# TensorE multiplies zeros in 32-row by 64-column tiles while the first rows load

## The chip, the cores and the metric

The kernel runs as one program on one core of a Trainium2 chip. The metric is the device time in microseconds (us) of that core, as the median of several runs. Beside it stands one profiled execution, from which all rows below are taken. TensorE (PE in the rows; its weight loads are PEld), VectorE (DVE), ScalarE (ACT), GpSimd (POOL) and SyncE (SP, which issues the DMAs here) each run their own instruction stream and meet at semaphores.

## The reference, cut to what matters

Two layers, each an attention-like part and a mixture of experts, over x of 4 sequences x 1024 rows x 256 columns:

```python
x = L0_attn_x                                   # (4, 1024, 256), float32
xn = _layernorm(x, axis=-1)
s = _L0_attn_ref(xn, ...)                       # layer norm again, Q, K, V, cumulative sum, gate
g = _silu(_L0_ffn_ref(xn, ...))                 # 16 experts by top-k of softmax(xn @ gate_w.T), and a shared one
x = x + s * g
xn = _layernorm(x, axis=-1)
s = _L1_attn_ref(xn, ...)                       # causal attention, 16 heads of 64, rotary positions
g = _silu(_L1_ffn_ref(xn, ...))                 # 8 experts, top 2
x = x + s * g
```

The change lies ahead of the first `_layernorm`. The zeros that it multiplies are used by nothing.

## The kernel before, in words

`build` runs stages one after the other: `normalize` (both layer norms of layer 0, and the gate's logits), `first_layer`, `experts`, `attention`, `moe`, `attention`. Between stages all engines meet at a barrier. Only `normalize` is changed; it takes the first 52 us.

`normalize` works in four batches b of 8 tiles of 128 rows (batch 0 in two halves), with these streams, each in written order:

- SP issues the loads: two halves of batch 0 of x (L162), four constants (L164), three more batches of x (L166). Later it issues the stores of the normalized rows (L173) and the loads of layer 0's weights (L170).
- VectorE, per batch: `statistics` (L190, L193, L196), then `rescaled` of the batch before (L220), then `staged` of its own (L209). `rescaled(b)` waits for `scaled_ps` 4b (L216), which TensorE raises when it has turned the scaled tiles of batch b-1; `staged` waits for GpSimd's reciprocal roots and, from batch 2 on, for `stage_ps` 4(b-1). In the end it copies the logits (L238).
- GpSimd computes the roots (L253 to L257, L268 to L270).
- TensorE, per batch: `turn_stage` (16 transposes of 128x128 by multiplication with the identity, L290), `logits` (8 x 2 multiplications, L299), `turn_scaled` (16 transposes, L310). Its first instruction waits for the four constants (L273 to L275), then `turn_stage` waits for `stage_made`.
- ScalarE evicts the turned tiles from PSUM (L326, L332).

A float32 multiplication by data appears in the trace as two weight loads and two MATMUL records; a transpose appears as one of each. A multiplication whose operands start at partition 0, 32, 64 or 96 and whose output covers only part of the partitions uses only that part (tile) of the array. `attention` does this for its heads: L1539 uses tiles of 64 rows by 128 columns, L1561 of 128 rows by 64 columns, L1571 of 64 rows by 128 columns; in each two tiles alternate.

`Scope.start` raises every semaphore of a stage by one, shared out over the five engines in turn, and then lets all engines meet. `normalize` has 20 of them before the change, four per engine.

Of the kernel before, what the change touches and what calls it, by code (L numbers as in the profile page):

```python
# [16 lines left out]
P = 128  # L17
# [9 lines left out]
ONE = 1  # L27
# [5 lines left out]
HEADS, DH = 16, 64  # L33
INNER = HEADS * DH
PAIRS = HEADS // 2
TB = T // P
# [82 lines left out]
def tiles(ap, n=TC):  # L119
    return ap.rearrange("p (t c) -> p t c", t=n)  # L120

def normalize(nc, d):
# [3 lines left out]
    with ExitStack() as ctx:  # L127
        s = Scope(nc, "n0", ctx)
# [11 lines left out]
        ps = s.banks()  # L140
# [5 lines left out]
        stage_ps, stage_read, scaled_ps, scaled_read = (s.sem(n) for n in ("stage_ps", "stage_read", "scaled_ps", "scaled_read"))  # L146
        log_ps, xn_out = s.sem("log_ps"), s.sems("xn_out")
        LOG = ps[6:8]

        def rows8(dram, b):  # L150

            return dram[b * T:(b + 1) * T, :].rearrange("(t p) c -> p t c", p=P)
# [5 lines left out]
        with nc.Block() as block:  # L158
            @block.sync
            def _(sp):  # L160
                for half, sem in ((0, x_half), (1, x_in[0])):
                    sp.dma_start(tiles(x[:, half * HT * C:(half + 1) * HT * C], HT), rows_of(d.x, half)).then_inc(sem, 16)  # L162
                for dst, src in ((ident, d.ident), (gate_w, d.gate_w["n0"]), (gain, d.gain["n0"]), (off, d.off["n0"])):
                    sp.dma_start(dst[:, :], src).then_inc(consts, 16)  # L164
                for b in range(1, QT):
                    sp.dma_start(tiles(part(x, b), GT), rows8(d.x, b)).then_inc(x_in[b], 16)  # L166
                for b in range(QT):
                    if b == 2:
                        for dst, src in d.l0_loads:
                            sp.dma_start(dst[:, :], src).then_inc(d.l0_in, 16)  # L170
                    u = b % 2
                    sp.wait_ge(stage_made, b + 2 + ONE)
                    sp.dma_start(rows8(d.xn["n0"], b), tiles(stage[u][:, :], GT)).then_inc(xn_out[u], 16)  # L173
                for u in range(2):
                    sp.wait_ge(xn_out[u], 16 * QT // 2 + ONE)
                sp.wait_ge(d.l0_in, 16 * len(d.l0_loads) + ONE)

            @block.vector
            def _(dve):
                st = Steps(dve, steps)  # L180

                def do(ins):
                    st.done(ins)
                    st.wait()

                def statistics(n):
                    at, wide = PARTS[n]
                    cols = slice(at, at + wide)
                    for i in range(at, at + wide):
                        st.done(dve.bn_stats(stats[:, i * 6:i * 6 + 6], x[:, i * C:(i + 1) * C]))  # L190
                    st.wait()
                    for i in range(at, at + wide):
                        st.done(dve.bn_aggr(mv[:, i * 2:i * 2 + 2], stats[:, i * 6:i * 6 + 6]))  # L193
                    st.wait()
                    var = mv[:, :].rearrange("p (t m) -> p t m", m=2)[:, cols, 1]
                    dve.tensor_scalar(v[:, cols], var, EPS, None, ALU.add).then_inc(var_made, 1)  # L196

                def staged(n):
                    at0, wide = PARTS[n]
                    b = at0 // GT  # L200
                    u = b % 2
                    dve.wait_ge(r_made, n + 1 + ONE)
                    if b >= 2:
                        dve.wait_ge(xn_out[u], 16 * (b // 2) + ONE)
                        dve.wait_ge(stage_ps, 4 * (b - 1) + ONE)
                        dve.wait_ge(scaled_made, b - 1 + ONE)
                    for at in range(at0, at0 + wide):
                        i = at % GT
                        ins = dve.tensor_scalar(stage[u][:, i * C:(i + 1) * C], x[:, at * C:(at + 1) * C],  # L209
                                                mv[:, 2 * at:2 * at + 1], r[:, at:at + 1], ALU.subtract, ALU.mult)  # L210
                    ins.then_inc(stage_made, 1)

                def rescaled(b):
                    u = b % 2
                    dve.wait_ge(r2_made, b + 1 + ONE)
                    dve.wait_ge(stage_made, b + 2 + ONE)  # L216
                    dve.wait_ge(scaled_ps, 4 * b + ONE)
                    for i in range(GT):
                        at = b * GT + i
                        ins = dve.tensor_scalar(scaled[u][:, i * C:(i + 1) * C], stage[u][:, i * C:(i + 1) * C],  # L220
                                                r2[:, at:at + 1], None, ALU.mult)
                    ins.then_inc(scaled_made, 1)

                dve.wait_ge(x_half, 16 + ONE)
                statistics(0)
                dve.wait_ge(x_in[0], 16 + ONE)
                statistics(1)
                staged(0)
                staged(1)
                for b in range(1, QT):  # L230
                    dve.wait_ge(x_in[b], 16 + ONE)
                    statistics(b + 1)
                    rescaled(b - 1)
                    staged(b + 1)
                rescaled(QT - 1)
                dve.wait_ge(log_ps, QT + ONE)
                for b in range(QT):
                    dve.tensor_copy(d.logits[:, :].rearrange("p (i b e) -> p b i e", b=B, e=E0)[:, b],  # L238
                                    LOG[b // 2][:, b % 2 * GT * E0:(b % 2 + 1) * GT * E0].rearrange("p (i e) -> p i e", e=E0))

# [31 lines left out]

            @block.tensor  # L273
            def _(pe):
                pe.wait_ge(consts, 16 * 4 + ONE)  # L275

                def xn_turned(b, i, c):
                    at = c * N + b * T + i * P
                    return xnT[:, at:at + P]

                def turn_stage(b):
                    for j in range(4):
                        half, c = j // 2, j % 2
                        if c == 0:
                            pe.wait_ge(stage_made, (1 + half if b == 0 else b + 2) + ONE)
                        if 4 * b + j >= 3:
                            pe.wait_ge(stage_read, 4 * b + j - 2 + ONE)
                        for i in range(4):
                            at = (half * 4 + i) * C + c * P
                            last = pe.transpose(ps[(4 * b + j) % 3][:, i * P:(i + 1) * P], stage[b % 2][:, at:at + P], ident[:, :])  # L290
                        last.then_inc(stage_ps, 1)

                def logits(b):
                    for i in range(GT):
                        if i % 4 == 0:
                            pe.wait_ge(stage_read, 4 * b + 2 * (i // 4) + 2 + ONE)
                        at = (b % 2 * GT + i) * E0
                        for c in range(KC):
                            last = pe.matmul(LOG[b // 2][:, at:at + P], xn_turned(b, i, c), gate_w[:, c * P:(c + 1) * P], start=c == 0, stop=c == KC - 1)  # L299
                    last.then_inc(log_ps, 1)  # L300

                def turn_scaled(b):
                    pe.wait_ge(scaled_made, b + 1 + ONE)
                    for j in range(4):
                        half, c = j // 2, j % 2
                        if 4 * b + j >= 3:
                            pe.wait_ge(scaled_read, 4 * b + j - 2 + ONE)
                        for i in range(4):
                            at = (half * 4 + i) * C + c * P
                            last = pe.transpose(ps[3 + (4 * b + j) % 3][:, i * P:(i + 1) * P], scaled[b % 2][:, at:at + P], ident[:, :])  # L310
                        last.then_inc(scaled_ps, 1)

                for b in range(QT):
                    turn_stage(b)
                    logits(b)
                    turn_scaled(b)
# [24 lines left out]
def renormalize(d, s, ps, gel, gel_done, stage, scaled, turned):  # L341
# [23 lines left out]
    scaled_late = s.sem("scaled_late")  # L365
    LOG = ps[7]

# [33 lines left out]
    def vector(dve):  # L401
# [56 lines left out]
        dve.wait_ge(log_ps, G + ONE)  # L458
        dve.tensor_tensor(out=te(d.sc), in0=LOG[:, 0:W].rearrange("p (t e) -> p t e", e=E1), in1=over_t(br), op=ALU.add)
        late_evicted(G - 1)  # L460
# [32 lines left out]
    def tensor(pe):  # L493
# [9 lines left out]
        def logits(g):  # L503
            pe.wait_ge(stage_read, 2 * g + 2 + ONE)
            for i in range(GT):
                at = (g * GT + i) * E1
                for c in range(KC):
                    last = pe.matmul(LOG[:, at:at + P], turned[g % 2][c][:, i * P:(i + 1) * P], gate_w[:, c * P:(c + 1) * P],
                                     start=c == 0, stop=c == KC - 1)
# [1685 lines left out]
```

## Time and profile before

| | us |
|---|---|
| three runs | 2538.72, 2538.75, 2542.49 |
| median | 2538.75 |
| span of the profiled execution, from first to last instruction | 2537.7 |
| TensorE busy in it | 2427.7 (96%) |
| VectorE, ScalarE, GpSimd busy | 1315.6, 1106.0, 606.3 |
| first MATMUL starts | 12.32 |
| last MATMUL of `normalize` ends | 50.23 |

The span is 1.05 us short of the median, which is what lies around the program. The mean granted clock of TensorE over the span is 0.982 of full speed. A busy time is the union of its records, so two records that run beside each other count once. The chain of waits of the page covers only 12% of the span and none of `normalize`, so for this stage the order of time and the waits of each engine are read instead.

### The profile page before, as it was taken

Reading aid. Unit: us, or ns where it says so; the run is one execution under the profiler, and the core shown is the slowest. Engines: PE = TensorE matmul, PEld = TensorE weight load, DVE = VectorE, ACT = ScalarE, POOL = GpSimd, SP = SyncE. Lnnn points to the kernel's source line nnn. Section 1 sums busy time; section 2 is a strip of 40 time slices with the busy share of each in tenths; the row PEclk is TensorE's granted clock in tenths of the full one; section 3 lists DMA queues with packets and bytes.
Section 4 is the critical chain, followed back from the end, with each engine's and each line's share of the span. In section 5 each row is a group of like instructions: output and inputs, shape, how many; then the busy total and the mean of one; then the engine's idle time right before and its main releaser. Section 6 shows DMA issues by size and latency. Waiting matters only on the chain. (4 is left out here: it accounts for less than half of the span.)

```text
span 2537.7 us, 45251 instructions
## 1 busy us (share of the span) xinstructions
PE 2427.7 (96%) x14680; PEld 1710.2 (67%) x14681; DVE 1315.6 (52%) x3690; ACT 1106.0 (44%) x2581; POOL 606.3 (24%) x535
## 2 busy tenths in 40 slices
PE   6999998999987899999999999999999999799997
PEld 5555555655566566666666666666899999566665
DVE  6666241222246766666666666655333333366665
ACT  3211111111125566666666666666222222266665
POOL 3002001444445233432111111110111111134341
PEclk9999999999988999999999999999999999899999
DMA  6013103975446232332111222122767666324231
GB/s 213 17 50 116 50 17 108 274 213 161 116 125 218 63 98 81 106 97 73 40 35 42 58 67 56 44 58 78 252 234 244 234 243 234 107 73 128 90 96 59
DMA packets 133965, 296.05 MB, mean 117 GB/s; under 512 B 16864, under 2 KB 87024, under 8 KB 123472
## 3 DMA queue, kind: packets, MB, share of 16 engines
q1 hardware_dynamic: 112896, 251.59, 31.0%
q0 software_dynamic: 20944, 42.94, 6.4%
q8 instruction: 60, 0.98, 0.2%
q14 instruction: 65, 0.53, 0.1%
HBM read 193.80 MB, written 67.12 MB: 103 GB/s over the span
## 5 line engine op out<-in xcount | busy, mean ns | idle before, releaser
L1595 ACT ACTIVATE at_p<-at_p,at_nmax 128x640 f32<-128x640 f32 (+7 forms) x512 | 392.5, 767 | 179.5 <-DVE at_nmax L1804 177.7
L1630 POOL TENSOR_TENSOR kept_big<-kept_xg 128x1024 f32<-128x1024 f32 x64 | 151.0, 2359 | 899.5 <-DVE kept_xg L1824 899.5
L1602 ACT ACTIVATE at_pT<-at_ps 128x512 f32<-128x512 f32 (+1 forms) x640 | 311.3, 573 | 106.2 <-PE at_ps L1547 106.1
L1804 DVE CUSTOM_DVE_ANT_0 at_p<-at_ps,atk_mask 128x512 f32<-128x512 f32 (+3 forms) x512 | 281.8, 585 | 143.7 <-PE at_ps L1539 143.5
L1547 PEld LDWEIGHTS at_ps<-kept_ident,at_p 128*128 128x128 f32 x2304 | 257.7, 142 | 111.5 <-issue 60.2
L1547 PE MATMUL at_ps<-kept_ident,at_p 128*128 128x128 f32 x2304 | 304.4, 278 | 11.4 <-ACT at_p L1595 10.8
L1539 PE MATMUL at_ps<-kept_big 64*128 64x512 f32 (+3 forms) x1536 | 298.7, 507 | 10.2 <-POOL kept_big L1630 6.5
L1561 PE MATMUL at_ps<-at_pT,at_v 128*64 128x256 f32 (+1 forms) x2560 | 270.2, 362 | 2.5 <-issue 2.5
L1839 DVE SCALAR_TENSOR_TENSOR kept_big<-at_ps,at_inv,kept_big 128x256 f32<-128x256 f32 x512 | 214.1, 475 | 89.1 <-issue 67.8
L1524 PE MATMUL at_ps<-atk_h,atk_w 128*128 128x512 f32 x512 | 240.8, 604 | 17.8 <-SPq L1338 17.8
L1561 PEld LDWEIGHTS at_ps<-at_pT,at_v 128*64 128x64 f32 x2560 | 174.0, 137 | 116.1 <-issue 29.3
L1038 PE MATMUL ex_ps<-kept_big 128*128 128x512 f32 x480 | 211.0, 598 | 0.9 <-ACT kept_big L1095 0.9
L1944 PEld LDWEIGHTS moe_ps<-moe_xT,moe_w 128*128 128x128 f32 x1696 | 197.5, 192 | 3.8 <-ACT moe_xT L1977 0.7
L1944 PE MATMUL moe_ps<-moe_xT,moe_w 128*128 128x128 f32 x1696 | 198.1, 275 | 0.5 <-ACT moe_xT L1977 0.5
L1539 PEld LDWEIGHTS at_ps<-kept_big 64*128 64x128 f32 x1536 | 128.3, 188 | 82.8 <-issue 47.6
L1038 PEld LDWEIGHTS ex_ps<-kept_big 128*128 128x128 f32 x480 | 92.1, 192 | 111.1 <-issue 110.4
L1100 ACT ACTIVATE kept_big<-ex_ps 128x512 f32<-128x512 f32 x64 | 38.2, 597 | 291.2 <-PE ex_ps L1038 269.0
L1524 PEld LDWEIGHTS at_ps<-atk_h,atk_w 128*128 128x128 f32 x512 | 92.1, 195 | 99.2 <-issue 80.9
L1922 POOL DMA_INDIRECT z_rows<-late_yo,late_to x71 | 68.8, 969 | 374.4 <-DVE late_yo L2005 374.4
L1804 DVE CUSTOM_DVE_ANT_0 at_p<-at_ps,atk_mask,at_nmax 128x128 f32<-128x128 f32 (+3 forms) x256 | 135.1, 546 | 27.9 <-PE at_ps L1539 27.9
L1824 DVE TENSOR_TENSOR kept_xg<-kept_xg,atk_cos 128x1024 f32<-128x1024 f32 x64 | 78.1, 1220 | 127.3 <-DMA kept_xg<-kept_xg 127.3
L1124 DVE TENSOR_TENSOR kept_big<-kept_big,ex_ps 128x512 f32<-128x512 f32 x64 | 44.0, 687 | 188.0 <-ACT kept_big L1100 188.0
(244 smaller groups left out, 3419.2 us busy)
## 6 DMA issues: line engine op xcount, KB each, us to landing
moe_w<-in_w_w SPq DMA_DIRECT2D x53, 1028.0 KB, 4.8
kept_xg<-kept_xg SPq DMA_DIRECT2D x256, 128.0 KB, 2.3
atk_first_w<-in_w_w SPq DMA_DIRECT2D x18, 1028.0 KB, 4.8
atk_w<-in_w_qkv SPq DMA_DIRECT2D x32, 384.0 KB, 3.1
slot_in<-kept_big SPq DMA_DIRECT2D x9, 1032.0 KB, 9.4
kept_big<-in_w_eg SPq DMA_DIRECT2D x16, 512.0 KB, 3.5
kept_big<-in_w_eu SPq DMA_DIRECT2D x16, 512.0 KB, 5.0
kept_big<-in_w_ed SPq DMA_DIRECT2D x16, 512.0 KB, 6.9
```

The costliest lines, as they stand in the source:

```text
L1038: last = pe.matmul(bank, w[:, k * F0 + f * P:k * F0 + (f + 1) * P], xT[u][k][:, :], start=k == 0, stop=k == KC - 1)
L1524: last = pe.matmul(banks[0], w[x][:, k * QKV + m * P:k * QKV + (m + 1) * P], h[:, k * T + half * CH:k * T + (half + 1) * CH], start=k == 0 ...
L1539: pe.matmul(banks[e][:, 0:to - at], qkT[x][e * DH:(e + 1) * DH, n * P:(n + 1) * P], qkT[x][e * DH:(e + 1) * DH, T + at:T + to], start=True ...
L1547: last = pe.transpose(banks[0][:, (i - 4 * j) * P:(i - 4 * j + 1) * P], p[(2 * t + e) % LAG][:, k * P:(k + 1) * P], ident[:, :])
L1561: last = pe.matmul(banks[0][e * DH:(e + 1) * DH, skip:QW], v[x][:, (k * 2 + e) * DH:(k * 2 + e + 1) * DH], pT[n][:, at + skip:at + QW], st ...
L1595: act.activation(buf, buf, ACT.Exp, bias=nmax[:, unit:unit + 1], scale=-1.0, accum_out=rsum[:, unit:unit + 1]).then_inc(exp_done, 1)
L1602: act.activation(dst, ring[RING_BANK[part][ev]][:, 0:(i1 - i0) * P].rearrange("p (k c) -> p k c", c=P), ACT.Copy).then_inc(t_read, 1)
L1630: pool.tensor_tensor(out=qkT[x][:, :].rearrange("p (m t) -> p m t", m=2)[:, :, half * CH:(half + 1) * CH], in0=raw[half][:, :].rearrange(" ...
L1804: ins = dve.tensor_tensor_reduce(out=p[unit % LAG][:, at:to], in0=ring[RING_BANK[part]["S", ((t, c), e), ahead]][:, 0:to - at], in1=mask[: ...
L1824: dve.tensor_tensor(out=both, in0=both, in1=table[:, half * CH:(half + 1) * CH].unsqueeze(1).to_broadcast([P, 2, CH]), op=ALU.mult).then_i ...
L1839: dve.scalar_tensor_tensor(out=part_y, in0=bank[:, t * C:(t + 1) * C], scalar=inv[:, unit:unit + 1], in1=part_y, op0=ALU.mult, op1=ALU.add ...
L1944: last = pe.matmul(bank[:, m * P:(m + 1) * P], w1[q][:, at:at + P], xT[u][:, k * P:(k + 1) * P], start=k == 0, stop=k == KC - 1)
```

## The change

Two buffers of 1024 columns, `blank` and `turned_blank`, and two semaphores are added. VectorE, ahead of its first wait for x, fills `blank` with zeros and turns it into `turned_blank` with two transposing instructions of 512 columns each, which turn blocks of 32 by 32. TensorE, ahead of its wait for the constants, waits for both of them and then does 3 x 8 x 8 = 192 multiplications: in step k, for each of two column halves e and four row groups a, weights of 32 rows by 64 columns, moving data of 32 rows by 256 - 32k columns. Row group a writes bank `ps[a]`, half e its partitions 64e to 64e+63. `turn_stage` later overwrites these banks with its own results.

```diff
+        blank, turned_blank = s.sb("blank", TB * P), s.sb("turned_blank", TB * P)
+        blank_made, blank_turned = s.sem("blank_made"), s.sem("blank_turned")
+        QR = P // 4
...
+                dve.memset(blank[:, :], 0.0).then_inc(blank_made, 1)
+                dve.wait_ge(blank_made, 1 + ONE)
+                dve.transpose(turned_blank[:, 0:4 * P].rearrange("p (k b c) -> p b k c", b=4, c=QR),
+                              blank[:, 0:4 * P].rearrange("p (k b c) -> p b k c", b=4, c=QR)).then_inc(blank_turned, 1)
+                dve.transpose(turned_blank[:, 4 * P:TB * P], blank[:, 4 * P:TB * P]).then_inc(blank_turned, 1)
                 dve.wait_ge(x_half, 16 + ONE)
                 statistics(0)
...
             def _(pe):
+                pe.wait_ge(blank_turned, 2 + ONE)
+                for step in range(3 * TB):
+                    k = step % TB
+                    for e in range(2):
+                        for a in range(4):
+                            rows = slice(a * QR, (a + 1) * QR)
+                            pe.matmul(ps[a][e * DH:(e + 1) * DH, k * QR:TB * QR], turned_blank[rows, e * DH:(e + 1) * DH],
+                                      turned_blank[rows, P + k * QR:P + TB * QR], start=k == 0, stop=k == TB - 1)
                 pe.wait_ge(consts, 16 * 4 + ONE)
```

TensorE's stream at its start, before the change (the shape is that of the output; a row with x16 stands for 16 instructions):

```order
L290 MATMUL n_ps<-kept_ident,n_stage 128x128 x16
L299 MATMUL n_ps<-n_gate_w,kept_big 128x128 x16
L310 MATMUL n_ps<-kept_ident,n_scaled 128x128 x16
L290 MATMUL n_ps<-kept_ident,n_stage 128x128 x16
```

And after it (all lines of the kernel lie lower, so L306 is the L290 of before):

```order
L289 MATMUL n_ps<-n_turned_blank 64x256 x8
L289 MATMUL n_ps<-n_turned_blank 64x224 x8
L289 MATMUL n_ps<-n_turned_blank 64x192 x8
L289 MATMUL n_ps<-n_turned_blank 64x160 x8
L289 MATMUL n_ps<-n_turned_blank 64x128 x8
L289 MATMUL n_ps<-n_turned_blank 64x96 x8
L289 MATMUL n_ps<-n_turned_blank 64x64 x8
L289 MATMUL n_ps<-n_turned_blank 64x32 x8
```

These eight rows stand three times, ahead of `L306 MATMUL n_ps<-kept_ident,n_stage 128x128 x16`; everything behind keeps its order.

VectorE's stream at its start, after the change; the first three rows are new, the fourth is its first row of before:

```order
L227 MEMSET n_blank 128x1024
L229 STREAM_TRANSPOSE n_turned_blank<-n_blank 128x4x4x32
L231 STREAM_TRANSPOSE n_turned_blank<-n_blank 128x512
L193 BN_STATS n_stats<-n_x 128x6 x4
L196 BN_AGGR n_mv<-n_stats 128x2 x4
```

Nothing else moves on VectorE, and ScalarE's, GpSimd's and SP's streams keep their order.

## Rows read from the trace of the kernel before

**Rows 1.** The page: span, busy time, clock by fortieths.
```profile
span 2537.7 us, 45251 instructions
PE 2427.7 (96%) x14680; PEld 1710.2 (67%) x14681; DVE 1315.6 (52%) x3690; ACT 1106.0 (44%) x2581; POOL 606.3 (24%) x535
PEclk9999999999988999999999999999999999899999
```

**Rows 2.** Order of time, TensorE, 0 to 54: start, duration, what, idle time before.
```profile
12.32 1.94 PE L290 MATMUL n_ps<-kept_ident,n_stage 128*128 128x128 f32 x8 [12.32 <-DVE n_stage L209]
14.55 2.01 PE L290 MATMUL n_ps<-kept_ident,n_stage 128*128 128x128 f32 x8 [0.28 <-DVE n_stage L209]
16.35 4.19 PE L299 MATMUL n_ps<-n_gate_w,kept_big 128*128 128x128 f32 x32
20.38 2.13 PE L310 MATMUL n_ps<-kept_ident,n_scaled 128*128 128x128 f32 x16
23.82 2.00 PE L290 MATMUL n_ps<-kept_ident,n_stage 128*128 128x128 f32 x16 [1.31 <-DVE n_stage L209]
...
33.07 2.00 PE L290 MATMUL n_ps<-kept_ident,n_stage 128*128 128x128 f32 x16 [1.43 <-DVE n_stage L209]
...
42.59 2.00 PE L290 MATMUL n_ps<-kept_ident,n_stage 128*128 128x128 f32 x16 [1.70 <-DVE n_stage L209]
44.43 3.83 PE L299 MATMUL n_ps<-n_gate_w,kept_big 128*128 128x128 f32 x32
48.10 2.13 PE L310 MATMUL n_ps<-kept_ident,n_scaled 128*128 128x128 f32 x16
53.75 0.45 PE L649 MATMUL l_ps<-wide_c_B,wide_c_A 8*128 8x256 f32 x1 [3.53 <-PEq L102]
```

**Rows 3.** Waits, 0 to 52: who waited for whom, total, times, longest.
```profile
DVE n_stats L190 <- DMA n_x<-in_x: 6.3, 1, 6.3
DVE n_stage L209 <- POOL n_r L257: 4.5, 5, 1.2
DVE wide_logits L238 <- PE n_ps L299: 2.4, 1, 2.4
DVE n_scaled L220 <- POOL n_r L257: 1.2, 1, 1.2
```

**Rows 4.** Windows, TensorE alone: stretch, length, busy (instructions), granted clock, DMA.
```profile
16.00:17.00 1.00, 1.00 (x7) 1.00 1.10 350
17.00:18.00 1.00, 1.00 (x9) 1.00 1.09 384
18.00:19.00 1.00, 1.00 (x11) 1.00 1.08 385
...
51.00:52.00 1.00, 0.00 (x0) 1.00 0.00 0
```

**Rows 5.** Order of time, other engines: loads, VectorE's first work, its later waits on TensorE.
```profile
2.53 0.99 SPq L162 DMA_DIRECT2D n_x<-in_x  x2
2.53 0.12 POOL L249 MEMSET n_expo<- 128x32 f32 x1 [2.07 <-POOLq L102]
6.41 1.40 DVE L190 BATCH_NORM_STATS2 n_stats<-n_x 128x6 f32<-128x256 f32 x4 [6.26 <-DMA n_x<-in_x]
...
27.21 2.19 DVE L220 TENSOR_SCALAR n_scaled<-n_stage,n_r 128x256 f32<-128x256 f32 x8
```

**Rows 6.** VectorE's groups by shape, or by line: duration of one.
```profile
L789 DVE TENSOR_TENSOR l_probs<-wide_logits,l_top 128x512 f32<-128x512 f32 x1 | 0.7, 693 | 0.0
L805 DVE MEMSET l_ones<- 128x512 f32 x1 | 0.5, 485 | 0.0
L1713 DVE MEMSET kept_big<- 128x2048 f32 x2 | 3.5, 1765 | 15.9 <-PEq L102 15.9
```

**Rows 7.** TensorE's groups by shape: rows*columns of the tile, busy, mean of one.
```profile
L1046 PE MATMUL ex_ps<-kept_big 128*128 128x256 f32 x480 | 106.1, 379 | 0.0
L1561 PE MATMUL at_ps<-at_pT,at_v 128*64 128x256 f32 x2048 | 247.7, 384 | 2.5 <-issue 2.5
L1571 PE MATMUL at_ps<-atk_wo,at_oT 64*128 64x256 f32 x1024 | 129.9, 383 | 0.0
```

**Rows 8.** Windows at a fresh start of L1539 (two row tiles), that line alone.
```profile
core 0: us, PE busy (x) PEld busy (x), PEclk, DMA share, GB/s
828.95:828.97 0.02, 0.00 (x0) 0.01 (x1) 1.00 0.29 102
828.97:828.99 0.02, 0.00 (x0) 0.02 (x1) 1.00 0.33 102
828.99:829.00 0.01, 0.01 (x2) 0.01 (x2) 1.00 0.06 0
829.00:829.17 0.17, 0.17 (x2) 0.17 (x4) 1.00 0.17 60
829.17:829.23 0.06, 0.06 (x4) 0.06 (x5) 1.00 0.19 68
```

## The prediction

> **What bounds the kernel now.** I read the page first. TensorE is busy for 2427.7 of 2537.7 us [rows 1], so over the whole program it is the bound. But the change touches only the first stage, and there I read TensorE's order of time, then the waits of the other engines, then narrow windows for the clock.
>
> TensorE's order of time [rows 2] shows three things. It does nothing until 12.32. Its first eight transposes take 1.94 us, where later sixteen take 2.00: 0.243 us each against 0.125, a factor of 1.94. And it idles before each later batch, for 1.31, 1.43 and 1.70 us, always until VectorE's `n_stage`. So batches 1 to 3 start when VectorE is ready, every 9.3 to 9.5 us, and TensorE has work for only about 7.6 us of them (42.59 to 50.23 for the last). The windows [rows 4] show where the factor of 1.94 ends: 7 instructions in the microsecond from 16, 9 in the next, 11 in the one after. The clock rose near 17.4, some 5.1 us after TensorE began. The granted clock reads 1.00 in these rows too, but it has no entry before its first change, so here the durations tell that TensorE was at the lower level (1.2 GHz) until then and at 2.4 GHz after.
>
> The waits [rows 3] say who sets the pace of the stage. VectorE waits for the first DMA until 6.41, then for GpSimd's roots (4.5 and 1.2 us), and for TensorE once, at the very end, for the logits. No wait of VectorE on `stage_ps` or `scaled_ps` shows. So the stage runs DMA, VectorE and GpSimd until 42.59, and from there TensorE's last batch at full clock, then ScalarE's last eviction. The slow clock of batch 0 lies off this path: batch 0 ends at 22.51 (20.38 + 2.13), 1.31 us before TensorE can go on. At full clock it would have ended 2.5 us earlier and waited 2.5 us longer.
>
> **The change, part by part.**
>
> *Semaphores.* 22 instead of 20 means that two engines raise five instead of four before all meet. The whole opening up to the first load at 2.53 [rows 5] holds four such steps and several meetings. One more is between 0 and 0.5 us (a fifth of the opening); I take 0.2 us, and it shifts the first load, so it is on the path.
>
> *VectorE.* It is free from 2.53 to 6.41 [rows 5]. A fill of 512 columns takes 485 ns and one of 2048 takes 1765 [rows 6], 0.83 ns a column, so 1024 columns take 0.91 us. No transposing instruction of VectorE is in the trace. From below it can't be less than nothing; from above the two-operand work on 512 columns takes 0.69 us [rows 6], and four times that would be 2.8 us. I take 0.69 for each of the two, since it is the nearest row in size. Sum: 2.53 + 0.91 + 2 x 0.69 = 4.8, with the handover to TensorE 4.9. Idle time before x arrives covers it, with 1.5 us to spare. If a transpose took over 1.45 us, the excess would delay x's statistics and the whole stage, one for one; at 2.8 us each that is 2.7 us.
>
> *TensorE.* 192 multiplications of a float32 pair are 384 MATMUL records and 384 weight loads. A record of 256 columns on the full array takes 106.1 / 480 = 221 ns at full clock [rows 7], 0.863 ns a column, and 1.94 times that at the lower level. The widths of one round of eight steps sum to 1152. If all eight tiles of a step run beside each other, a step lasts two records: 2 x 0.863 x 1152 = 1.99 us a round, 6.0 us for three at full clock, 11.6 us at the lower one.
>
> Do eight tiles run beside each other? What the trace shows is two. L1561 (two column tiles) spends 247.7 / 2048 = 121 ns on a record of 256 columns, L1571 (two row tiles) 127 ns, against 221 alone [rows 7]. How they get there stands in the windows of a fresh start of L1539 [rows 8]. The first tile's load begins between 828.95 and 828.97; by 829.00 two loads and two MATMULs have begun, while no third MATMUL begins until after 829.17. The two that began are the first halves of both tiles: the second tile did not wait for the first one's second half. So work is handed to each tile as it comes, and the fifth instruction of the stream was out less than 0.05 us after the first, under 12 ns for each. At that rate the 32 instructions of a step are out in under 0.4 us, about the 0.44 us that the widest step lasts at full clock and half its length at the lower. So I take eight beside each other, and the bounds are 11.6 us for that and four times as much, 46 us, for two beside each other, both at the lower clock.
>
> The Trainium skill, "TensorE: Matmul & The Clock Gate", Part 3, says that small tiles run concurrently, 16 of them in the length of one and 4 ns for each further one, 10.6 times faster than in turn. By it the sum would stay as it is.
>
> When does the clock rise? From its first instruction at 12.32 it took TensorE 5.1 us [rows 2, 4]. If it is the same here: 5.1 us at the lower level do 5.1 of the 11.6, the other 6.5 / 1.94 take 3.4, and TensorE is free at 4.9 + 8.5 = 13.4. If the thin tiles never raise it, it is free at 4.9 + 11.6 = 16.5.
>
> What that delay costs follows from the slack. VectorE's `rescaled(1)` at 27.21 [rows 5] needs batch 0 turned, and the last batch must start at 42.59. TensorE needs about 8.0 us a batch when it runs without pause (7.6, and some 0.4 while ScalarE is still evicting), so batch 0 has to be done by 42.59 - 16.0 = 26.6. At full clock (7.6 us) it may start at 19.0, at the lower (22.51 - 12.32 = 10.2 us) at 16.4. Starting at 13.4 costs nothing; starting cold at 16.5 costs 0.1. I take 0.1.
>
> *What is gained.* At most the 2.5 us of batch 0, and they end in TensorE's wait for `n_stage`. Behind 50.23 TensorE idles until 53.75 [rows 2, 4] in both kernels, so whatever clock it was given is gone by the next stage. I take 0.
>
> Sum: 2537.7 + 0.2 + 0.1 = 2538.0 for the span, and with the 1.05 us around it 2539.0, against the median of 2538.75.
>
> **The rivals.**
>
> *A: instructions can't be issued that fast (the case on the other side: slower).* In the same windows [rows 8] the first MATMUL begins no sooner than 828.99, 20 to 50 ns after its load, and I took that for a latency. If some 31 ns of it were the price of each instruction, 768 of them would take 23.8 us whatever the clock. TensorE would be free at 28.7, batch 0 done at 36.3 (or 38.9 cold), the last batch would start 16.0 later, at 52.3 to 54.9 instead of 42.59: 9.7 to 12.3 us more, some 2549.8. Below 18 ns an instruction (13.8 us in all) it costs nothing; from there on each further ns costs 0.77 us. Against it speaks the fifth instruction within 0.05 us; for it, that the trace has no long run in which the tiles would not be the limit.
>
> The Trainium skill has such a price in the same page, Part 1, "Wait — 56ns, not 53.3ns?": some 62 ns for each MATMUL if the sequencer's own code decodes it. An estimate by that page is 384 x 62 = 23.8 us, and the time again near 2550. Four MATMULs of two tiles within 0.23 us of the first load [rows 8] don't exclude it, because they are few.
>
> *B: only two tiles run beside each other.* The row sums [rows 7] show no more than two. Then 5.1 us at the lower clock and (46.4 - 5.1) / 1.94 = 21.3 at the higher: free at 31.3, batch 0 done at 38.9, the last batch at 54.9: 12.3 us more, 2551. One at a time would be twice the work, 52 us, and some 2577. Against it: the second tile's start in [rows 8] needs nothing from the first, and I see no reason for a third to.
>
> *C: the warm start pays.* If some wait on TensorE in batch 0 were on the path after all, up to 2.5 us would come back: 2536.5. VectorE's waits [rows 3] speak against it. Even then it is below what counts as faster.
>
> *D: the code lies elsewhere.* TensorE's program grows by 768 instructions, and where its loops begin in their loaded pieces shifts, on VectorE too. No row prices this; I leave 3 us to both sides.
>
> **How the numbers follow.** A measurement of this kernel can tell a change from none at about 0.2%, or 5.1 us. Forecast (0 to 3 us more or less, with C and most of D inside): 0.72. A, and rates between 18 and 31 ns that cost part of it: 0.11, of which 0.03 stays below 5.1 us. B: 0.08; one at a time 0.02; VectorE's transposes late 0.02, still below 5.1 us. A faster kernel by more than 5.1 us has no mechanism in these rows; I leave 0.05, for D. So faster 0.05, slower 0.08 + 0.08 + 0.02 = 0.18, same 0.77. The likeliest case alone spans 2535.5 to 2542. For eight in ten the range takes in the late transposes and the cheaper half of A and stops short of B: 2535 to 2547. The time is that of the forecast, 2539.0.
>
> **What would show it right or wrong.** VectorE's fill at 2.5 to 3.5 and two transposes ending before 5.2, its L193 still at 6.4 to 6.6. TensorE's L289 rows beginning near 4.9 and ending between 13 and 17, with a busy time near 8.5 to 11.6 us; ending near 28 speaks for A, and there the steps of 256 and of 32 columns would last equally long; ending near 31, with steps that shrink with their width, for B. L306 of the last batch near 42.8, and no new wait of VectorE for L326 at its L223. The forecast is wrong if TensorE's last batch starts after 45, or if the time moves by over 5 us with that start in place, which would be D.

## The result, and the profile after

The changed kernel took 2542.91 us, the median of 13 runs, against 2538.75 of 13 runs of the kernel before: ratio 1.0018, 95% interval 1.0010 to 1.0025. Run again in the same rounds as later variants it took 2540.5 (11 runs) against 2539.05 (35 runs): 1.0005, 0.9997 to 1.0014. So by the medians it is slower by 1.5 to 4 us, less than the 5.1 us that I had called the least that can be told from none; the second interval alone does not exclude none. The forecast of 2539.0 was too low by 3.9 us, inside its range. One execution of a later variant (one round) took 6122.13 us at a granted clock of 0.396, and its ratio leaves it out.

The profiled execution has a span of 2543.8 us and took 2545.57, which is 2.7 above the median. In every run on record the time is 1.72 to 1.86 us above the span of the same execution, so the profiled execution of before, with its span of 2537.7, took an estimated 2539.5, 0.7 above its median. Span against span is therefore 6.1 us, more than the medians show.

Here is TensorE's order of time after, which answers to [rows 2]:

```profile
5.12 5.72 PE L289 MATMUL n_ps<-n_turned_blank 32*64 32x256 f32 x217 [5.12 <-DVE n_turned_blank L231]
14.46 4.16 PE L289 MATMUL n_ps<-n_turned_blank 32*64 32x96 f32 x128 [3.62 <-issue]
19.57 0.72 PE L289 MATMUL n_ps<-n_turned_blank 32*64 32x96 f32 x39 [0.94 <-issue]
20.23 1.53 PE L306 MATMUL n_ps<-kept_ident,n_stage 128*128 128x128 f32 x12
22.91 0.66 PE L306 MATMUL n_ps<-kept_ident,n_stage 128*128 128x128 f32 x4 [1.16 <-ACT kept_big L342]
...
29.04 1.47 PE L306 MATMUL n_ps<-kept_ident,n_stage 128*128 128x128 f32 x12
...
45.30 1.47 PE L306 MATMUL n_ps<-kept_ident,n_stage 128*128 128x128 f32 x12
47.30 0.65 PE L306 MATMUL n_ps<-kept_ident,n_stage 128*128 128x128 f32 x4 [0.53 <-ACT kept_big L342]
47.79 3.84 PE L315 MATMUL n_ps<-n_gate_w,kept_big 128*128 128x128 f32 x32
51.47 2.13 PE L326 MATMUL n_ps<-kept_ident,n_scaled 128*128 128x128 f32 x16
```

The zeros keep TensorE busy for 5.72 + 4.16 + 0.72 = 10.6 us, as forecast (8.5 to 11.6). But they come in three pieces of 217, 128 and 39 records. Between them TensorE stands idle for 3.62 and 0.94 us, ended by "issue": nothing that the profile shows released it. So it is free at 20.2, not at 13.4 to 16.5. Batch 0 then takes 8.8 us up to the next batch's start, each later one 8.13, and the last starts at 45.30 instead of 42.59. The stage's last MATMUL ends at 53.60 instead of 50.23, and the next stage's first begins at 57.24 instead of 53.75, 3.5 us later. The other 2.6 of the 6.1 us come behind this stage, in code that the change does not touch: the start of `experts` is 4.0 us later (399.29 against 395.32), that of the second `attention` 5.0 (2199.70 against 2194.74).

The other engines' order of time, around the first zeros and the first eviction:

```profile
2.82 0.91 DVE L227 MEMSET n_blank<- 128x1024 f32 x1 [2.67 <-PEq L102]
3.76 0.71 DVE L229 STREAM_TRANSPOSE n_turned_blank<-n_blank 128x512 f32<-128x512 f32 x1
4.40 0.67 DVE L231 STREAM_TRANSPOSE n_turned_blank<-n_blank 128x512 f32<-128x512 f32 x1
6.15 1.41 DVE L193 BATCH_NORM_STATS2 n_stats<-n_x 128x6 f32<-128x256 f32 x4 [1.08 <-DMA n_x<-in_x]
...
20.97 1.28 ACT L342 ACT_TABLE_LOAD   x1 [20.97 <-PE n_ps L306]
```

VectorE's fill took 0.91 us and its transposes 0.71 and 0.67, against 0.91 and 0.69 assumed, and x's statistics began at 6.15, no later than before. ScalarE loads a table, 1.28 us, when its first tile is ready, and TensorE, which may fill three banks ahead, waits 1.16 us for ScalarE. Before, this load stood at the same place in ScalarE's stream (13.49, also 1.28 us), but there TensorE had time to spare.

VectorE's waits, which answer to [rows 3]:

```profile
DVE n_scaled L223 <- PE n_ps L326: 4.4, 2, 2.4
DVE wide_logits L246 <- PE n_ps L315: 3.9, 1, 3.9
```

The first row is new: twice `rescaled` waited for TensorE's turned tiles, 4.4 us in all. The stage is now bound by TensorE from 20.2 on.

What TensorE did while it was idle, and in the pieces around, shows in the windows (busy and count of PE, PEld, DVE, ACT, POOL, then granted clock, DMA share, GB/s):

```profile
7.00:10.84 3.84, 3.84 (x189) 3.59 (x177) 3.26 (x17) 0.00 (x0) 2.18 (x6) 1.00 1.07 332
10.84:14.46 3.62, 0.00 (x0) 0.00 (x0) 2.69 (x9) 0.00 (x0) 2.96 (x9) 1.00 1.08 350
14.46:18.60 4.14, 4.13 (x128) 3.94 (x128) 3.97 (x20) 0.00 (x0) 2.61 (x6) 0.59 1.09 360
18.60:19.57 0.97, 0.03 (x3) 0.00 (x0) 0.97 (x5) 0.00 (x0) 0.97 (x1) 1.00 0.82 284
```

In the first idle stretch the DMA engines are full with x's loads, at 350 GB/s. The clock's 1.00 in the first two rows says little, since its record has no entry before the first change. The durations tell that the zeros raised it: the 16 records of 256 columns took 0.91 us in the first round (5.12 to 6.03), and 0.44 in the second (8.79 to 9.23). It fell soon after the idle stretch: over 15.00 to 18.40 the granted clock is 0.50, and over the whole second piece 0.59. And the DMA queues of the stretch from 0 to 13 hold one row that the stretch from 0 to 11.9 lacks (queue: packets, MB, share of 16 engines):

```profile
q1 hardware_dynamic: 3492, 3.14, 74.7%
q8 instruction: 1, 0.02, 0.5%
```

```profile
q8 instruction: 1, 0.02, 1.4%
```

The kernel before had none in its first 20 us. Its first began at 29.26, when TensorE had begun 225 MATMULs and weight loads. The second piece of zeros has exactly 128 records, with their weight loads 256 instructions, which would be 64 bytes of a packet for each. That is theory L (late code): TensorE ran out of loaded instructions, and the next 256 came late, behind x's loads.

### The profile page after: what moved, and what is told of

Same layout as the page of the kernel before. It is cut to its first block and busy times, and to the rows that moved or that the text cites. A ratio compares the mean times of both kernels' runs of the same rounds, so it can differ in the third digit from the quotient of the medians.

```text
span 2543.8 us, 46024 instructions
## 1 busy us (share of the span) xinstructions
PE 2438.4 (96%) x15064; PEld 1719.4 (68%) x15065; DVE 1318.2 (52%) x3693; ACT 1105.9 (43%) x2581; POOL 606.4 (24%) x535
```

## The experiments

Each kernel ran against the kernel before on the same chip: the first four in one group of rounds, the next four in a second, the last four in a third. Compare ratios across the groups, not medians. Theory L has two rivals: W, the streaming of the zeros itself or the tiles' overlap costs the time; K, only the clock at the next stage's start fell differently. Ratios are to the kernel before, with 95% intervals.

| kernel | median us | ratio | interval |
|---|---|---|---|
| one round | 2538.69 | 0.9995 | 0.9986 to 1.0004 |
| narrow | 2540.85 | 1.0001 | 0.9992 to 1.0010 |
| few wide | 2536.73 | 0.9989 | 0.9980 to 0.9998 |
| table first | 2541.78 | 1.0005 | 0.9996 to 1.0014 |
| loads later | 2546.47 | 1.0022 | 1.0013 to 1.0031 |
| before, loads later | 2540.39 | 0.9998 | 0.9989 to 1.0006 |
| before, end filled | 2538.76 | 0.9998 | 0.9989 to 1.0007 |
| before, both filled | 2537.97 | 0.9996 | 0.9987 to 1.0004 |
| the change again | 2540.50 | 1.0005 | 0.9997 to 1.0014 |
| narrow again | 2542.81 | 1.0011 | 1.0003 to 1.0020 |
| few wide again | 2536.85 | 0.9989 | 0.9980 to 0.9997 |
| short and filled | 2535.66 | 0.9985 | 0.9976 to 0.9994 |

Single executions of any of these scatter by about 3 us either way, so the traces carry the argument on the place and the ratios that on the price.

**One round.**

```diff
-                for step in range(3 * TB):
+                for step in range(TB):
```

> One round of eight steps instead of three: 256 of the 768 added instructions. Theory L (late code: TensorE idled 3.62 us from 10.84 and 0.94 us from 18.6 for nothing that the profile shows, while a 16 KB packet of its code queue began only at 11.97 under full DMA queues): no idle time inside L289, its end near 9, first real transpose near 12.1 as before the change, last batch at 42.3 to 42.7, and no cost: 0 to 0.3 us over before, ratio 1.000. Theory W (the streaming work itself or the tiles' overlap costs): a third of the work, a third of the loss, +1.4 us. Theory K (the clock at the next stage's start fell differently, and that is the loss): a change of 0 to 2 us either way, with L677 beginning at another clock and nothing lost before 50.

TensorE's order of time:

```profile
5.12 4.33 PE L289 MATMUL n_ps<-n_turned_blank 32*64 32x256 f32 x128 [5.12 <-DVE n_turned_blank L231]
12.51 1.26 PE L306 MATMUL n_ps<-kept_ident,n_stage 128*128 128x128 f32 x8 [3.07 <-DVE n_stage L212]
...
42.72 2.00 PE L306 MATMUL n_ps<-kept_ident,n_stage 128*128 128x128 f32 x16 [1.70 <-DVE n_stage L212]
```

One unbroken piece, free at 9.5, last batch at 42.72, no loss. As L expected, and against W. K is weakened too: the clock was low from 54.2 to 61.0 in this execution, twice as long as before, and its span was 2538.6, 0.9 above that of before. With the change the clock was low there for as long, 6.8 us, so K may hold part of what comes behind the stage (0.5 us by the start of `experts`), but not the 3.5 that are there before it.

**Narrow, twice.** All multiplications have the width of the last step.

```diff
-  pe.matmul(ps[a][e * DH:(e + 1) * DH, k * QR:TB * QR], ...
-            turned_blank[rows, P + k * QR:P + TB * QR], ...
+  pe.matmul(ps[a][e * DH:(e + 1) * DH, 7 * QR:TB * QR], ...
+            turned_blank[rows, P + 7 * QR:P + TB * QR], ...
```

> The same 192 multiplications and 768 instructions, every one only 32 columns wide, so 2.3 us of streaming where the change has 11.6 at the lower clock. Theory L: the code still can't be there; TensorE uses up what is loaded within some 2 us, idles from near 7 for 5 us or more in all, and L289 ends at 16 to 19; cost 1 to 4 us over before. Theory W: L289 ends near 8 to 9 and the time is that of before.

> All multiplications 32 columns wide, 768 instructions, again. Theory L: its first real transpose began at 19.95 as the change's did at 20.23, so it must cost as much as the change does, within 1.5 us. Were the streaming work the cost (theory W), it would cost at least 3 us less than the change.

TensorE's order of time in the first of them:

```profile
5.12 3.27 PE L289 MATMUL n_ps<-n_turned_blank 32*64 32x32 f32 x217 [5.12 <-DVE n_turned_blank L231]
12.93 2.04 PE L289 MATMUL n_ps<-n_turned_blank 32*64 32x32 f32 x128 [4.53 <-issue]
19.13 0.89 PE L289 MATMUL n_ps<-n_turned_blank 32*64 32x32 f32 x39 [4.16 <-issue]
19.95 2.79 PE L306 MATMUL n_ps<-kept_ident,n_stage 128*128 128x128 f32 x12
```

The pieces have the same sizes, 217, 128 and 39. The busy time fell from 10.6 to 6.2 us, the idle time rose from 4.6 to 8.7, and TensorE was free at 19.95, nearly as late as with the change. W is refuted as to the place: it is not the streaming that sets the end, but the number of instructions. Here too each piece began 1.3 to 1.5 us after the end of a q8 packet (10.48 to 11.61, and 16.53 to 17.65); over the six profiles with 768 added instructions that holds for all twelve restarts. In the rounds that they share, narrow (1.0011) was not cheaper than the change (1.0005), though W wanted it 3 us cheaper. The first time it was dearer than before by less than could be resolved.

The first piece answers the rival on issue, too: 217 MATMULs and their 217 loads in 3.27 us are 7.5 ns for an instruction. And these thin zeros left the clock low: the first 12 transposes behind them took 2.79 us, against 1.53 with the change.

**Few wide, twice.** Instead of the loops:

```diff
+                for step in range(10):
+                    pe.matmul(ps[step % 4], turned_blank[:, 0:P], turned_blank[:, 4 * P:TB * P], start=True, stop=True)
```

> Ten multiplications of 128 rows by 128 columns with 512 moving columns instead of the 192 small ones: 40 instructions, busy time about 5 us cold and 6 us warm, 11 us, as long as or longer than the change's 10.6. Theory L: one unbroken run from 5.1 to about 16, no idle time inside, the last batch at 42.3 to 43, no cost: 0 to 0.5 us over before. Theory W: the same loss as the change, +4 us.

> Ten wide multiplications, 40 instructions, again. The first time it came out 2.2 us below before, with an interval of 0.5 to 5 us, and its profile gave no cause in this stage (last batch at 43.03 against 42.59). If that was scatter: within 1.5 us of before. If it is real: 1.5 to 3 us below before again.

```profile
5.12 11.08 PE L285 MATMUL n_ps<-n_turned_blank 128*128 128x512 f32 x20 [5.12 <-DVE n_turned_blank L231]
16.04 1.47 PE L301 MATMUL n_ps<-kept_ident,n_stage 128*128 128x128 f32 x12
...
33.51 2.07 PE L301 MATMUL n_ps<-kept_ident,n_stage 128*128 128x128 f32 x16 [0.42 <-DVE n_stage L212]
...
43.03 3.00 PE L301 MATMUL n_ps<-kept_ident,n_stage 128*128 128x128 f32 x16 [1.70 <-DVE n_stage L212]
```

More busy time than the change's, in 40 instructions: one piece, free at 16.0, and by batch 2 TensorE waits for VectorE again. The place is as L expected. That it is faster than before, 0.9989 both times, was not expected, and nothing in this stage explains it: in the first profile the last batch starts 0.44 us later than before, the clock falls in it, and the next stage begins at 55.76, 2.0 us later than before.

The profiles place the gain far behind. The second `attention` takes 339.7 us from its first MATMUL to the end of the program in four profiles (both of few wide, the second of narrow, short and filled), and 342.9 to 344.2 in the other ten. The four lack two stretches at the lower clock that the others have, near 2212 and near 2495. Before, and few wide again:

```profile
2208.00:2222.00 14.00, 10.74 (x38) 5.56 (x39) 5.91 (x19) 6.03 (x19) 6.56 (x3) 0.76 0.62 213
2490.00:2510.00 20.00, 16.04 (x110) 10.84 (x108) 12.57 (x40) 12.34 (x30) 5.35 (x3) 0.91 0.26 83
```

```profile
2208.00:2222.00 14.00, 11.29 (x64) 6.70 (x64) 6.49 (x20) 8.26 (x24) 5.98 (x3) 1.00 0.64 213
2490.00:2510.00 20.00, 15.04 (x108) 9.64 (x108) 13.43 (x46) 14.74 (x34) 5.53 (x3) 1.00 0.26 86
```

These 3.3 us and more are larger than the gain of 2.2. All three profiles with a wide start are among the four, and one of the eleven others, a slow kernel. Whether the wide start brings this about, and by what path, no run shows.

**Table first.**

```diff
+                act.wait_ge(blank_made, 1 + ONE)
+                act.activation(warm[:, :], blank[:, 0:1], ACT.Copy)
                 act.wait_ge(consts, 16 * 4 + ONE)
```

> The change with one ScalarE copy of a single column ahead of its first wait, so that its table of 1.28 us is loaded near 4 and not at 20.97, between the first turned tile and its eviction. Theory T (table and late code add up): batch 0 takes TensorE 7.7 to 8.0 us instead of 9.0, last batch at 44.0 to 44.4 instead of 45.30, time 1.0 to 1.3 us below the change, some 3 us over before. If the table is no part of the path: the same time as the change, last batch at 45.3.

ScalarE's order of time, and TensorE's:

```profile
2.53 1.28 ACT L338 ACT_TABLE_LOAD   x1 [2.53 <-PEq L102]
```

```profile
14.47 2.50 PE L290 MATMUL n_ps<-n_turned_blank 32*64 32x96 f32 x128 [3.06 <-issue]
20.12 1.04 PE L290 MATMUL n_ps<-n_turned_blank 32*64 32x96 f32 x39 [3.15 <-issue]
21.10 3.01 PE L307 MATMUL n_ps<-kept_ident,n_stage 128*128 128x128 f32 x16
```

The table is out of the way and TensorE's 1.16 us of waiting in batch 0 are gone. But the second piece, at full clock this time, was done sooner and only waited longer for its code (3.15 us), the clock was low again at 21.10, and the last batch came at 45.73, not at the 44.0 to 44.4 expected. Its ratio, 1.0005, is that of the change run again. So the table's place in the chain is seen, its price is not settled.

**Loads later, and its control.** In the change, and by itself in the kernel before:

```diff
                 for b in range(1, QT):
+                    if b == 2:
+                        sp.wait_ge(stage_made, 1 + ONE)
                     sp.dma_start(tiles(part(x, b), GT), rows8(d.x, b)).then_inc(x_in[b], 16)
```

> The change with the loads of x's batches 2 and 3 issued only after the first stage tiles are made (near 12), so that the DMA queues are empty between the end of batch 1's load (some 10 us) and then. Theory L: the 16 KB packet of TensorE's code starts 1 to 3 us sooner than 11.97 and the first idle time inside L289 shrinks from 3.62 to 0 to 2 us; L289 ends near 16 to 18.5; cost against the kernel before 0 to 2 us instead of 4. If the queues' load has no part in it: the packet at 12 and 3.6 us idle as in the change.

> Control for the run with later loads: the kernel before with the same later loads and no zeros. Batches 2 and 3 are wanted at 23.7 and 32.9 and land near 15 and 18.5, so 0 us over before, within 0.05%; were the later loads of use or harm by themselves, that would show here.

TensorE's order of time with the change, and the windows of its two idle stretches:

```profile
13.10 2.50 PE L291 MATMUL n_ps<-n_turned_blank 32*64 32x96 f32 x128 [2.33 <-issue]
20.67 1.05 PE L291 MATMUL n_ps<-n_turned_blank 32*64 32x96 f32 x39 [5.07 <-issue]
```

```profile
10.77:13.10 2.33, 0.00 (x1) 0.00 (x1) 1.40 (x5) 0.00 (x0) 1.87 (x6) 1.00 0.10 28
15.60:20.67 5.07, 0.00 (x0) 0.00 (x0) 4.24 (x21) 0.00 (x0) 3.29 (x9) 0.76 0.96 305
```

The first code packet began at 10.57, where it was 11.97 with the change, and the first idle time shrank from 3.62 to 2.33 us, with the DMA engines at a share of 0.10. Even so it did not vanish: the three profiles of these widths with the loads in place have 3.06 to 3.62 us, so waiting behind x's loads accounts for 0.7 to 1.3 us of it, and the rest is there with DMA engines nearly empty.

The second idle time grew from 0.94 to 5.07, and I had looked only at the first. Two things make it up. The second piece ran at full clock and ended at 15.60, 3.0 us sooner than with the change; table first, with the loads in their old place, shows that alone (2.50 us for the piece, then 3.15 idle). And the packet for the third piece began 5.13 us after the second piece, under the delayed loads (18.23 to 19.21), where it was 2.79 to 4.31 us in the other five profiles with 768 added instructions. So the packet's end sets the restart, as L says, but how much of its lateness is x's loads is settled for the first stretch alone. In all there is more idle time, 7.4 us against 4.6, and the kernel lost 0.22%. The control, 0.9998, shows no price of the loads' new place by itself.

**End filled, both filled.** Two short bursts at full width: in the first kernel behind the last turned tile, in the second also between the stages.

```diff
                     turn_scaled(b)
+                pe.matmul(ps[0], ident[:, :], xnT[:, 0:CH], start=True, stop=True)
+                pe.matmul(ps[1][:, 0:2 * P], ident[:, :], xnT[:, 0:2 * P], start=True, stop=True)
...
         HB = NCH // 2
+        nc.tensor.matmul(ps[0], ident[:, :], d.xnT[:, 0:CH], start=True, stop=True)
+        nc.tensor.matmul(ps[1][:, 0:P], ident[:, :], d.xnT[:, 0:P], start=True, stop=True)
         s.start()
```

> The kernel before, with one and a half multiplications of 512 columns behind its last turned tile, while ScalarE still evicts (50.23 to 51.5), so TensorE's idle time before the next stage is 2.3 us instead of 3.5. The result is unused. If the clock's fall at 54.8 hangs on that idle time, the next stage's first matmuls run at full clock more often: 0 to 1.7 us faster than before. If 2.3 us are still enough for the fall: the same time.

> As the run with the filled end, and a second short burst between the two stages while TensorE's sequencer raises the semaphores of the next stage. TensorE is then idle for at most about 1 us at a stretch: the clock stays at its higher level through 55 to 58, 1.0 to 1.7 us faster than before (ratio 0.9993 to 0.9996), less up to 0.3 us if the burst holds up the barrier. If the clock falls all the same: the same time or 0.3 us slower.

With the end alone, TensorE was still idle for 2.24 us, and the clock was low from 53.9. With both it was never idle for a full microsecond around the barrier (0.86 and 0.30), and the next stage began at full clock, though its first own MATMUL came at 54.69 instead of 53.75. Neither difference in time is clear of nothing (0.9998, 0.9996).

**The change again.** The same file as the changed kernel.

> The change itself, in the same rounds as the narrow and the wide variant, since single executions scatter by some 3 us and their first intervals overlap. Theory L: TensorE idles inside L289 for 4 to 5 us again and frees itself at 20 to 21; +2.5 to +5 us over before.

The pieces were 217, 128 and 39 once more, with 3.34 and 4.25 us idle, more than the 4 to 5 expected in all, and TensorE free at 22.75, not at 20 to 21. Its price, 1.0005 or 1.5 us, was below the 2.5 us expected, with an interval that reaches 1.0014. In its profile the next stage began at 60.73, 7.0 us later than before, and the span, 2542.4, was 4.7 us longer. So a delay at this stage's end does not reach the end of the program one for one: in single executions the later stages differ by as much as the price in question.

**Short and filled.** Five wide multiplications at the start instead of ten, and both bursts.

```diff
-                for step in range(10):
+                for step in range(5):
```

> A version meant to beat both: five wide multiplications at the start (20 instructions, free before x's first tiles are made at 12.3) and the two short bursts around the barrier at the stage's end. The start brings nothing on the path, the fill keeps the clock up in the next stage's first 3 to 7 us: 1 to 2.5 us faster than before, ratio 0.9990 to 0.9996; below 0.9990 only if the wide start has a gain of its own.

It is faster than the kernel before, 0.9985, 0.9976 to 0.9994, 3.4 us under its median, where 1 to 2.5 were expected, and its median is 4.8 under the change's in the same rounds. From few wide (0.9989) it is not told apart. In its windows the two rows at the next stage's start have a granted clock of 1.00:

```profile
54.00:58.00 4.00, 3.70 (x12) 1.92 (x12) 2.70 (x5) 1.18 (x3) 0.00 (x0) 1.00 0.47 146
58.00:62.00 4.00, 4.00 (x10) 1.71 (x9) 2.26 (x8) 0.74 (x2) 0.00 (x0) 1.00 0.35 119
```

In the same stretch of the kernel before the clock was 0.61 and 0.97:

```profile
54.00:58.00 4.00, 4.00 (x8) 1.86 (x8) 3.20 (x6) 0.72 (x2) 0.00 (x0) 0.61 0.63 214
58.00:62.00 4.00, 4.00 (x10) 1.71 (x9) 1.50 (x7) 1.19 (x2) 0.00 (x0) 0.97 0.15 50
```

The lower level lasted 3.4 us there, so the higher one gives back an estimated 1.7, while the bursts let the stage's own first MATMUL start 0.75 later (54.50 instead of 53.75). In this profile 1.6 us are gained by the start of `experts` (393.76 against 395.32), and 3.2 in the second `attention`, which is the gain of few wide with its open cause.

## Why the prediction was right or wrong

- *What bounds the stage, and that a warm start gains nothing there.* One round started batch 0 nearly when before did (12.51 against 12.32), left its last batch where it was (42.72), and its time can't be told from that of before. The rows had no place for a gain, and in this stage none came. Few wide is faster by 0.11% all the same, by a difference that its profiles show some 2150 us later.
- *Semaphores, 0.2 us.* The loads began at 2.53 in both. So no cost shows at the first load; only VectorE began 0.3 us later than the 2.53 that I had for it, at 2.82.
- *The 1.05 us around the span.* This term set one execution's span against the median of others. Within one execution it is 1.72 to 1.86, so the term was some 0.7 us too small.
- *VectorE, 4.9 us until TensorE may begin.* It was 5.12.
- *Streaming, 8.5 to 11.6 us, eight tiles beside each other.* 10.6 busy. At 217 MATMULs and their loads in 3.27 us (narrow) no price of 31 ns exists, and rival A is out. The Trainium skill, "TensorE: Matmul & The Clock Gate", Part 1, gives some 62 ns for a MATMUL where the sequencer's own code decodes it; this case's trace does not bear such a price, with 15 ns for a MATMUL and its load. Rival B is out too: a round took about 4 us at mostly the lower clock, where two tiles at a time would have taken 15. (The prediction's 52 us for one tile at a time should read 50.3 by its own rates, 5.1 + 87.7 / 1.94; it bears on nothing else.)
- *TensorE free at 13.4 to 16.5.* This is the step that failed. The sum "4.9 + 8.5" took the 768 instructions as present. They were not all there: 4.6 us of idle time between the pieces, each ended 1.3 to 1.5 us after a packet of code had arrived, put the end at 20.2. The prediction had named the code's place under D and priced it at plus or minus 3 us without a row. A row was there to ask for: the DMA queues of the kernel before, in which q8's first packet comes at 29.26, behind 225 of TensorE's MATMULs and loads, while the first 20 us are full with x.
- *Slack: a warm start until 19.0 is free.* Too kind by 1.5 us. From TensorE's start of batch 0 to that of batch 3 it took 25.07 us (45.30 - 20.23), not 7.6 + 16.0 = 23.6: the table load stands behind the first tile, and each later batch takes 8.13. So the limit was 42.59 - 25.07 = 17.5, and TensorE was 2.7 us past it. Its last batch took 8.30 instead of 7.64, since ScalarE no longer had a head start: 3.4 us at the stage's end, against 4.2 in the first median and 1.5 in the second.
- *Range and chances.* The time lay in 2535 to 2547. "Same" within 0.2% held by a small margin, and by luck: not because nothing was lost, but because what was lost came to a little less than that. The prediction's own sign of being wrong, TensorE's last batch after 45, came true at 45.30.

## What to carry to other kernels

Work that fills an engine's idle time needs its instructions loaded as well: here some 435 of the zeros' were there at the start, and each further 256 came by a DMA packet among the tensors' own. Fill with few, wide instructions. And a warm clock is worth something only where the engine sets the pace next: at this stage's start it gained nothing (one round), and behind its barrier an estimated 1.7 us by the profile, which the times of the kernels with bursts alone are too coarse to confirm. Last, a difference of 0.1% can come from the clock's course two milliseconds further on; compare the starts of all stages before crediting it to the change.

## What the runs showed of the hardware

- TensorE, at 7.5 ns an instruction, used up its loaded code in 3.3 us; the packet with the next 256 took about 1.1 us and the first of them ran some 1.4 us after it had ended, even with the DMA engines nearly empty (loads later: packet 10.57 to 11.68, first MATMUL at 13.10; the change: 11.97 to 12.99, and 14.46). The 7.5 ns and 3.3 us are narrow's.
- Eight tiles of 32 rows by 64 columns ran beside each other: 16 records of 256 columns took 0.91 us at the lower clock and 0.44 at the higher, twice the length of one alone at either (0.43, which is 1.94 x 0.221, and 0.221). TensorE's group by shape, with the change (busy, mean of one):

```profile
L289 PE MATMUL n_ps<-n_turned_blank 32*64 32x256 f32 x48 | 3.2, 568 | 5.1 <-DVE n_turned_blank L231 5.1
```

  48 records of 256 columns kept it busy for 3.2 us, part of that at the lower clock; one at a time would take 48 x 0.22 = 10.6 at full clock.
- Zeros in thin tiles raised the clock: the same 16 records took 0.91 us and then 0.44, and a fall to 0.50 is recorded after it. With 32 columns in each and more idle time between (narrow) they left it low, at 2.79 us for the first 12 transposes.
- A VectorE transpose of 512 float32 columns in blocks of 32 by 32 took 0.67 to 0.71 us, the longer time with a strided pattern.
